# A two-layer transformer kernel on one core: the experts' second pass spread over seven rounds instead of six, and layer 1's first sums and norms moved into the last round

## What is computed

```python
xn = layernorm(x)
# layer 0: full attention, 16 heads of 16, and 8 experts with a top-1 gate
qkv = xn @ W_qkv + b_qkv
attn = softmax(q @ k.T) @ v                       # per batch and head
aff = xn @ centroids.T; e = argmax(aff); alpha = sigmoid(aff[e])
h = relu(layernorm_e(xn) @ w1[e].T + b1[e])       # 256 -> 1024
y = xn + h @ w2[e].T + b2[e]                      # 1024 -> 256
x = x + attn + alpha * y + (1 - alpha) * xn
# layer 1
xn = layernorm(x)
attn1 = causal attention, its context through a 3-tap convolution into new queries,
        a second causal attention with the same k and v, and an output projection
P = xn @ U1; H = gelu(P @ V1 + b1); ffn1 = (H @ U2) @ V2 + b2
x = x + attn1 + ffn1
```

## Time and profile before

| | us |
|---|---|
| median of 3 runs | 1966.15 |
| lowest and highest | 1963.6, 1976.36 |
| the profiled execution's own time | 1965.93 |
| its span, first to last instruction | 1964.1 |
| mean granted TensorE clock (share of 2.4 GHz) | 0.966 |

### The profile page before, as it was taken

The page is one execution under the profiler, slowest core; times in us unless marked ns, Lnnn a source line. Parts: engine busy times, 40 slices in busy tenths (PEclk is TensorE's granted clock), DMA queues, the critical chain, the costliest instruction groups (busy, mean ns, idle before and its releaser), DMA issues.

```text
span 1964.1 us, 31719 instructions
## 1 busy us (share of the span) xinstructions
PE 1795.0 (91%) x10745; PEld 880.7 (45%) x10745; DVE 1254.4 (64%) x3788; ACT 1023.1 (52%) x2064; POOL 338.6 (17%) x525
## 2 busy tenths in 40 slices
PE   4868999999889999997789898999999999999987
PEld 2313555555344555541234344445554454545443
DVE  6675555555644555557553766778786777777673
ACT  1444565655546555655554344555554555555544
POOL 2222211121111222113443101101010101111000
PEclk7878999999989999998999899999999999999999
DMA  6655432343754443332105243655454455555330
GB/s 160 181 142 139 79 65 75 79 90 73 180 111 74 65 71 60 53 48 78 51 22 80 37 63 50 82 77 82 77 72 72 66 78 75 85 75 74 61 50 23
DMA packets 144654, 155.79 MB, mean 79 GB/s; under 512 B 24696, under 2 KB 131472, under 8 KB 144496
## 3 DMA queue, kind: packets, MB, share of 16 engines
q1 hardware_dynamic: 123584, 114.71, 35.5%
q0 software_dynamic: 9024, 14.42, 4.1%
q10 hardware_dynamic: 11888, 24.64, 3.8%
HBM read 55.93 MB, written 33.69 MB: 46 GB/s over the span
## 4 chain that ended last, share of the span: by engine, by line
PE 68%; DVE 11%; DMA 7%; SPq 5%; issue 4%; ACT 3%; POOL 2%; ACTq 0%; DVEq 0%; POOLq 0%
PE p_PV L1138 12%; PE p_S L1121 9%; PE p_S L1065 5%; PE p_S L1082 5%; SPq L2307 5%; PE p_Ma L1341 4%; DMA t_R<-t_msp 4%; PE p_Ma L1221 4%; PE p_S L1198 4%; DVE p_S L1509 3%; PE p_S L1125 2%; PE p_Ma L1364 2%; PE p_Mb L1198 2%; DVE t_mx L1495 1%; PE p_S L1221 1%
## 5 line engine op out<-in xcount | busy, mean ns | idle before, releaser
L1969 ACT ACTIVATE t_R<-p_S 128x512 f32<-128x512 f32 (+1 forms) x1216 | 682.4, 578 | 552.2 <-PE p_S L1125 396.8
L1509 DVE CUSTOM_DVE_ANT_0 p_S<-p_S,t_NM 128x128 f32<-128x128 f32 x1008 | 474.7, 515 | 201.4 <-PE p_S L1082 198.4
L1121 PE MATMUL p_S<-t_R 99*128 99x512 bf16 (+3 forms) x1536 | 475.2, 333 | 34.6 <-DMA t_R<-t_msp 17.3
L1495 DVE TENSOR_REDUCE t_mx<-p_S 128x1 f32<-128x512 f32 x512 | 347.9, 686 | 242.3 <-PE p_S L1065 240.1
L1138 PE MATMUL p_PV<-t_R 128*17 128x512 f32 (+3 forms) x3072 | 329.8, 502 | 1.2 <-issue 1.0
L1082 PE MATMUL p_S<-t_R 96*128 96x128 bf16 x1008 | 255.3, 305 | 19.1 <-DMA t_R<-t_spl 10.4
L1121 PEld LDWEIGHTS p_S<-t_R 99*128 99x128 bf16 x1536 | 150.9, 98 | 173.4 <-ACT t_R L1969 69.0
L1065 PE MATMUL p_S<-t_R 96*128 96x512 bf16 x512 | 202.1, 397 | 26.6 <-DVE t_mx L1495 16.2
L2171 POOL CAST t_spl<-t_rr 128x512 bf16<-128x512 f32 x80 | 49.5, 619 | 911.1 <-DVE t_rr L1467 911.1
L1125 PE MATMUL p_S<-t_NM 128*128 128x128 bf16 x1024 | 199.4, 220 | 0.0
L1509 DVE DVE_READ_ACCUMULATOR2_ANT t_mx<- 128x1 f32 x1024 | 143.9, 140 | 0.1
(11 more groups left out here) (282 smaller groups left out, 2157.2 us busy)
## 6 DMA issues: line engine op xcount, KB each, us to landing
t_R<-t_spl SPq DMA_DIRECT2D x480, 128.0 KB
t_R<-in_w ACTq DMA_DIRECT2D x32, 512.0 KB, 8.1
t_R<-ks SPq DMA_DIRECT2D x96, 128.0 KB
ks<-t_spl SPq DMA_DIRECT2D x16, 384.0 KB, 5.2
hTd<-t_NM SPq DMA_DIRECT2D x39, 128.0 KB
ysd<-t_NM SPq DMA_DIRECT2D x39, 128.0 KB
t_NM<-hTd SPq DMA_DIRECT2D x39, 128.0 KB, 2.5
ysd<-t_NM POOLq DMA_DIRECT2D x39, 128.0 KB, 3.1
```

What stands on the lines that cost most here:

```text
L1121: t = self.nc.tensor.matmul(bank[:, z, :], ka[0:99, h, kb * 128:(kb + 1) * 128], qa[0:99, h, n0:512], start=True, stop=not u.causal)
L1495: nc.vector.tensor_reduce(m.mx[:, g, 4 * j + qb:4 * j + qb + 1], m.S1[s1_bank(k)][:, :], AX.X, ALU.max).then_inc(s.s1_read, 1)
L1509: x = nc.vector.tensor_tensor_reduce(out=sc, in0=sc, in1=m.maskq[:, 512 - n:512], scale=1.0, scalar=NEG, op0=ALU.add, op1=ALU.max, accum_o ...
L1969: nc.scalar.activation(m.P1X[kb][j0 // per] if u.causal else m.P[p % 2][:, j0:j0 + per, :], m.s2_bank(k)[:, 0:per * n].rearrange("p (j n) ...
```

## The change

The second pass runs through rounds 8 to 14, 28 steps in each (before: 33 in rounds 8 to 12 and the rest in round 13). Round 14 has no gathers and no joined. Round 15 gets one lane: the gathers of batches 0 and 1, parts, joined(0), joined(1), the gathers of batches 2 and 3; before, it had turn_n(0) and turn_n(1), joined(2) with two groups of gathers, and parts, as three lanes. turn_n(0) now stands at the start of ffn, turn_n(1) in the first iteration of its loop. In the loop joined runs two batches ahead of far, before it was three; its wait for turn_n(b-2) then refers to an earlier iteration. The gathers stay four ahead.

```diff
@@ layer0
-        if 8 <= i < 14:
-            lanes.append(take(second, 33 if i < 13 else 80))
-        if i == 14:
+        if 8 <= i < 15:
+            lanes.append(take(second, 28 if i < 14 else 80))
+        if i == 15:
             e.arrivals_begin()
-            lanes.append(chain(e.gathers(0), e.gathers(1), e.joined(0), e.joined(1)))
-        if i == 15:
             e.load_layer1()
-            lanes += [chain(e.turn_n(0), e.turn_n(1)), chain(e.gathers(2), e.joined(2), e.gathers(3)), e.parts()]
+            lanes += [chain(e.gathers(0), e.gathers(1), e.parts(), e.joined(0), e.joined(1), e.gathers(2), e.gathers(3))]
         weave(e, *lanes)
@@ ffn
     e.ffn_begin()
-    interleave([(e.near(0), 1)])
+    for _ in chain(e.turn_n(0), e.near(0)):
+        pass
     for b in range(NB):
         lanes = [(e.far(b), 1)]
         if b >= 1:
             lanes.append((e.tail(b - 1), 1))
-        if b == 0:
-            lanes.append((e.near(1), 2))
-        elif b + 1 < NB:
+        if b + 1 < NB:
             lanes.append((chain(e.turn_n(b + 1), e.near(b + 1)), 2))
-        if b + 3 < NB:
-            lanes.append((e.joined(b + 3), 1))
+        if b + 2 < NB:
+            lanes.append((e.joined(b + 2), 1))
         if b + 4 < NB:
             lanes.append((e.gathers(b + 4), 1))
         lanes.append((e.ones_rows(b), 4))
```

## The result

| us | before | after |
|---|---|---|
| median of 4 runs each | 1969.43 | 1998.09 |
| lowest and highest | 1963.6, 1976.36 | 1987.59, 2001.7 |
| the profiled execution: time | 1965.93 | 1987.59 |
| its span | 1964.1 | 1985.1 |
| its mean granted clock | 0.966 | 0.965 |

The ratio of the two kernels, run in turns on one chip, is 1.0127 (95% interval 1.0102 to 1.0153): 20 to 30 us slower, where 9 were forecast (1975 us) and the range ended at 1993. The profiled execution is the fastest of the four; the clocks of the other three were 0.956, 0.961 and 0.954.

What follows compares the result with a forecast made beforehand. PE was taken to bound rounds 8 to 13, with idle PE time in round 14. The terms -17.3, +9.9 and +16.1 gave +8.7 us on 1965.93, so 1975 us, range 1953 to 1993.

Steps and rivals of the forecast that it cites:

- Part 1: Rounds 8 to 14: second pass spread over seven rounds, 28 steps moved into round 14's idle PE time; -17.3 us.
- s: Time of one step of the second pass in a PE-bound round: 0.78 us, bounds 0.70 to 0.83.
- 8.4-33s: Net of rounds 8 to 14: rounds 8 to 13 lose 28s, round 14 becomes 49.2-5s against 40.8; -17.3 us.
- Part 2: Round 15 to far(0): DVE's longer chain, then turn_n(0) and near(0); far(0) starts 43.0 us in against 33.1, +9.9 us.
- Part 3: Loop of ffn: with joined two batches ahead, PE waits for DVE's norms at turn_n; +16.1 us, bounds 0 to 21.6.
- The rival: Loop of ffn: granted clock falls at PE's new wait ahead of turn_n, 17 us over six iterations; 1992 us, chance 0.16.
- The rival of round 14: Round 14: the pass is bound by its own hand-overs and uses no idle time; 1992 us, chance 0.06.
- Loop free: Loop of ffn absorbs the moved chain, so part 3 costs nothing; 1958.5 us, as low as 1953.6, chance 0.20.
- Round 14 not filled: Round 14 grows by what the other rounds lose, 28*0.78 = 21.8 us; 1992 us, chance 0.06.
- Faster by over 1%: Whole kernel: only turn_n(0) is paid, the loop is free, s = 0.83; 1950 us or less, chance 0.06 (below 1946.5: 0.05).
- slower by over 1%: Whole kernel above 1985.8 us: chances 0.16 and 0.06 from two rivals, 0.03 from the forecast's own upper bounds; 0.25.

Runs made afterwards that it cites:

- six-round kernel: The changed kernel with the second pass back in six rounds (33 steps a round, 31 in round 13), all else as changed; 1.0144 to the kernel before.
- two ahead alone: The kernel before with joined(b+2) instead of joined(b+3) in the loop and joined(2) out of round 15; 1.0115, +22.6 us.
- filler in the loop: The changed kernel with 14 unread matmuls on PE ahead of turn_n's wait for the norms in iterations 1 to 5; 1.0111 to the kernel before.
- both waits filled: The changed kernel with unread matmuls on PE: 14 ahead of turn_n's wait, 40 in round 15 ahead of its wait for the first close; 1.0065 to before.
- repaired change: The changed kernel with joined(0) and joined(1) overlapped in round 15, norms three batches ahead, and normalizations moved into the next iteration; 1.0027 to the kernel before.
- late norms: The kernel before with joined(b+3) cut after 14 steps, its normalizations run in the next iteration behind five empty steps; 0.9984.
- three ahead: The changed kernel with joined(2) and joined(3) in iteration 0 and joined three batches ahead from there; 1.0058 to the kernel before, +11.4 us.

## Why the prediction was wrong

**Part 1, right, its price too high.** Rounds 8 to 13 lost 19.9 us for 28 steps, s = 0.71, not 0.78, within its bounds of 0.70 to 0.83. The forecast's own formula, 8.4-33s, gives -15.0 with it, and -15.0 was measured. That fit is in part luck: round 8 gave 5.3 of the 19.9 for five steps, some of it clock, and rounds 9 to 13, with the clock at 1.00 in both kernels, gave 14.6 for 23 steps, 0.63 a step and below the lower bound. Round 14 filled as drawn: 45.7 us, PE 45.1 of them, clock 1.00 (forecast 45.3). But the forecast gave the whole gain to PE work that fills idle time, and by the six-round kernel 7.4 us of it are there without the seventh round, where only the gathers and joins have left; it also shows that this round alone takes 33.4 us.

**Part 2, right in every order, 2.1 us short.** The close at 23.8 (24), PE's stop for it, POOL's 3.4 us ahead of the norms, far(0) at 45.1 (43.0). DVE's own chain kept its times: joined(0)'s last join ended 15.7 us in (15.5), its norms 23.4 (23.1), joined(1)'s norms 34.1 (34.0). The term that was off is PE's: its second half ran in part at half clock and ended at 35.1, not near 33, and the last close, waiting 2.13 us for it, started at 36.3 where 34.0 was forecast. The serial turn_n(0) took 2.7 us (940.57 to 943.25) where 3.3 were forecast, near(0) 5.3 instead of 5.0.

**Part 3 and the clock: here it failed.** The step that failed is the granted clock of the loop: the central sum put its cost at nothing and left it to a rival with a chance of 0.16. The reason given was that one round of like busy share had the clock at 1.00; but a round's busy share says nothing of a new wait at one place in each turn. The runs show that the clock falls behind that very wait, behind five of six in the change and all six with two ahead alone, and that it stays at 1.00 where the wait is filled. The rival was the forecast's own sum plus 17 us (1974.6 + 17 = 1992), so its term belonged in the central sum, at its measured size: 16.1 + 17 = 33 would have been too much for the loop's +25.0. PE's waits grew by 18.2 us (forecast 16.1), and the other 7 in this execution are no waits. From far(0) to layer 1's first exponential 23.3 us were at half clock after and 13.8 before; if half of the difference is lost, my estimate, that is 4.8 of the 7.

Iteration by iteration: near(2) came 5.0 us later relative to far(0) (forecast 2.8; with filler in the loop 3.4). Iterations 2 to 4 took 13.9 more (8.2; with filler 7.4, so the 2.3 and 3.6 of the forecast are borne out and the rest is the clock's). Iteration 5 took 3.8 more (3.6). Iteration 6 took 5.6 more where 1.5 were forecast; this is a second term that was mis-sized, and of the order, not of the clock alone:

```profile
1077.89 1.09 PE L993 MATMUL p_Ma<-t_ident,t_NM 128*128 128x128 f32 x4 [3.91 <-DVE t_NM L1452]
```

The norms of batch 7 end not "a little after" turn_n(7) wants them but 3.9 us after. Both filler kernels leave this wait unfilled, and it stands in them at 3.9 us as well, with iteration 6 as long (28.0 and 26.9 us, against 26.7 and, before, 21.1). Behind iteration 6, 3.3 us came back, where before had run 13.7 us at half clock (1093.5 to 1107.2) and after had none.

The price of the rival was 2.8 per iteration, from a third of the serial work at half rate; the filler measured 8.3 over four iterations, 2.1 each (4.6 over the whole loop in the trace of the kernel with both waits filled). By the timed ratios the clock is 12 of the 25 us, round 15 included, and the order 13, with the doubts said at that kernel. The rival's 1992 is +26 us, and the ratio measured is +25. In part that is luck: in the trace its -17.3, +9.9 and +33 were -15.0, +12.0 and +25.0. The rival of round 14 gave 1992 too, by a mechanism that round 14's row refutes.

The Trainium skill (TensorE: Matmul & The Clock Gate, section "HAM oscillation — how this bites in real kernels") says that a loop in which TensorE waits anew each turn can fall to half rate each turn. The trace agrees for five of the six: four of the waits for the norms are followed by 3.4 us at 1.2 GHz and one by 6.8 us.

**The rivals.** Loop free: refuted by two ahead alone, +22.6. Round 14 not filled: refuted by its row. Faster by over 1%: refuted. The chances for slower by over 1% (0.25) were too small for a change whose forecast had PE stand still seven times anew (once in round 15, six times in the loop).

**What stays open.** Why the half-clock time in round 15 differs between kernels that are one program up to there; the exact split of the 25 us between clock and order; what the serial turn_n(0) costs; and the 3 us between the repaired change or the late norms and the kernel before. No version here clearly beats the kernel before.

## What to carry to other kernels

When a schedule change makes the bounding engine wait once per turn of a loop, put a price on the slower clock behind the wait into the central sum, and not only into a rival. How far ahead a producer runs is worth as much as the work itself: two batches instead of three cost 22.6 us alone, more than the 15.0 that rounds 8 to 14 gave, which round 15 nearly paid back. To learn a clock's share, give the engine work that nobody reads in exactly that wait, in all such waits at once, and compare the timed ratios with both kernels side by side; a single trace may show the clock low elsewhere.

## What was unexpected in the hardware

- The half-clock stretch that began in round 15 was 10.2, 13.7 and 30.7 us long in three kernels that are one program up to there (three ahead, the change, filler in the loop), and 34.1 us in the six-round kernel; in the kernel before, where PE doesn't stand still for that close, there was none. The timed runs of the change spread (1987.6 to 2001.7), the longer ones with the lower clock (0.965 to 0.954).
- In the same loop, the clock fell behind five of the six waits of 3.4 to 3.9 us, and stayed at 1.00 beside the waits of 1.4 and 1.7 us per turn, and beside one of 2.8, in the kernel before.
- An attention round without any other work takes 33.4 us although its PE work is 27.5 and its DVE work 24.5 (3.4 us of it ran at half clock). That the hand-overs between the engines set it is my reading and wasn't tested; shown is that the emptied round gave back 7.4 us (40.8 to 33.4) and still lasts 5.9 us longer than its PE work.
